# An attention and gated-update kernel: token tiles split in token order and turned by DMA, x added in the last stage, and GpSimd adding both pairs of probability tiles in odd units only

## The reference, cut to what matters

```python
x = x + attention(layernorm(x), ctx, ctx)          # 32 query heads, 8 key heads, softmax over 512 keys
y = layernorm(x)
# ffn(y): gates over 8 experts, the largest one wins; a rank-8 update of y by its matrices
x = x + ((1 - gate) * y + gate * (bias + degen @ (update.T @ (y - debias))))
```

## Time and profile before

| | |
|---|---|
| median of three runs | 1025.13 us (1024.51 to 1025.3) |
| profiled execution: span from the first to the last instruction | 1023.9 us (no time beside the span is given for it) |
| TensorE matmul busy | 949.4 us, 93% |
| VectorE busy | 904.8 us, 88% |
| GpSimd busy | 794.4 us, 78% |
| ScalarE busy | 761.3 us, 74% |
| mean granted TensorE clock | 0.992 |
| DMA | 319876 packets, 164.19 MB, 182216 of them under 512 B |

### The profile page before, as it was taken

How to read it: one execution, slowest core, us unless ns; L and a number is a source line. 1 busy time by engine, 2 the same in 40 slices (tenths; PEclk the granted TensorE clock), 3 DMA queues, 4 the chain that set the end, 5 groups by cost and what they waited for, 6 DMA issues and landing times.

```text
span 1023.9 us, 24706 instructions
## 1 busy us (share of the span) xinstructions
PE 949.4 (93%) x9518; PEld 372.5 (36%) x9518; DVE 904.8 (88%) x1138; ACT 761.3 (74%) x1333; POOL 794.4 (78%) x422
## 2 busy tenths in 40 slices
PE   4789999999999999999999999999999999999996
PEld 3223233333333232333333333332222226777773
DVE  6869999999999999999999999998888876888976
ACT  7468888888888888888888888888777777554440
POOL 7158999999999999999999999998999998222110
PEclk9989999999999999999999999999999999999998
DMA  7675677767677767676767686766555744766423
GB/s 247 184 167 114 161 154 168 156 162 159 155 158 167 168 152 170 145 171 150 180 143 175 138 188 134 182 122 154 119 119 139 165 95 141 247 213 236 148 104 164
DMA packets 319876, 164.19 MB, mean 160 GB/s; under 512 B 182216, under 2 KB 307240, under 8 KB 319760
## 3 DMA queue, kind: packets, MB, share of 16 engines
q1 hardware_dynamic: 319456, 161.76, 64.3%
q0 software_dynamic: 304, 0.85, 0.3%
HBM read 107.58 MB, written 54.53 MB: 158 GB/s over the span
## 4 chain that ended last, share of the span: by engine, by line
PE 36%; DVE 30%; issue 25%; ACT 5%; POOL 2%; DMA 1%; SPq 0%; DVEq 0%; POOLq 0%; ACTq 0%
DVE row_max L949 14%; PE psum L589 8%; PE psum L603 6%; PE psum L616 5%; PE psum L734 5%; DVE den_t L961 4%; PE psum L551 4%; ACT probs L884 3%; PE psum L712 3%; DVE o_t L955 3%; PE psum L577 2%; DVE probs L1161 2%; DVE prod_mem L1008 2%; PE psum L700 1%; ACT prod_mem L824 1%
## 5 line engine op out<-in xcount | busy, mean ns | idle before, releaser
L884 ACT ACTIVATE probs<-psum 128x512 f32<-128x512 f32 x1024 | 554.7, 596 | 106.7 <-PE psum L589 88.7
L949 DVE TENSOR_REDUCE row_max<-psum 128x4 f32<-128x2048 f32 x248 | 566.0, 2282 | 63.5 <-PE psum L551 63.1
L589 PE MATMUL psum<-q_stack,k_stack 97*32 97x512 f16 x4096 | 335.0, 386 | 10.2 <-issue 3.6
L363 POOL TENSOR_TENSOR sums<-probs 128x2048 f32<-128x2048 f32 x63 | 287.8, 4568 | 19.5 <-ACT probs L884 19.5
L351 POOL TENSOR_TENSOR sums<-probs 128x2048 f32<-128x2048 f32 x63 | 287.2, 4558 | 10.2 <-PE psum L626 5.5
L603 PE MATMUL psum<-probs,v_in 128*32 128x512 f32 x2048 | 268.9, 598 | 1.0
L589 PEld LDWEIGHTS psum<-q_stack,k_stack 97*32 97x32 f16 x4096 | 96.8, 95 | 258.7 <-ACT probs L884 148.6
L551 PE MATMUL psum<-high_mem 32*128 32x512 f16 x992 | 98.3, 385 | 23.7 <-DVE row_max L949 20.0
L323 POOL TENSOR_TENSOR o_t<-o_t,inv 128x512 f32<-128x512 f32 x64 | 67.1, 1048 | 44.2 <-DVE inv L967 44.2
L328 POOL TENSOR_TENSOR o_all<-o_all,o_t 128x512 f32<-128x512 f32 x64 | 81.5, 1274 | 9.5 <-POOL o_t L323 0.4
L603 PEld LDWEIGHTS psum<-probs,v_in 128*32 128x32 f32 x2048 | 59.4, 111 | 61.1 <-issue 16.7
(11 more groups left out here) (120 smaller groups left out, 788.9 us busy)
## 6 DMA issues: line engine op xcount, KB each, us to landing
q_stack<-q_split SPq DMA_DIRECT2D x192, 128.0 KB, 3.4
xa<-in_x_dram SPq DMA_DIRECT2D x32, 512.0 KB, 4.7
o_all<-in_x_dram SPq DMA_DIRECT2D x256, 64.0 KB, 2.5
x_attended<-o_all SPq DMA_DIRECT2D x64, 256.0 KB, 4.1
out_dram<-probs SPq DMA_DIRECT2D x32, 512.0 KB, 2.9
q_split<-prod_mem SPq DMA_DIRECT2D x15, 1024.0 KB, 5.4
xa<-x_attended SPq DMA_DIRECT2D x16, 512.0 KB, 4.5
probs<-x_attended SPq DMA_DIRECT2D x16, 512.0 KB, 5.3
```

Source lines behind the costliest of these rows:

```text
L363: pool.tensor_tensor(sums[:, 2 * u % SUMS], probs[:, u % 2, 0], probs[:, u % 2, 1], ALU.add).then_inc(front_done, 1)
L589: last = pe.matmul(st_ps[row:row + D, bank_of["score", u, n], :], k_stack[:, u % SLOTS, t * P + row:t * P + row + D], q_stack[:, u % SLOTS ...
L884: act.activation(probs[:, s, keys, g, :], st_ps[:, bank_of["score", u, n], :], ACT.Exp, scale=EXP_SCALE).then_inc(exped, 1)
L949: dve.reduce_max(row_max[:, u % 2, t:G * ST:ST], s_ps[:], AX.X).then_inc(reduced, 1)
```

## The change

- **Tiles from the sixth on** (n = 5 to 31) no longer go through TensorE and PSUM. ScalarE scales and rounds the context (`split_context`), normalises x in place in one pass (`normalise_tile`) and copies it to f16 (`high_part`), at fixed places among the exponentials: before numbers 4 and 6 of even units and 2 of odd ones. GpSimd subtracts for the low parts (`low_parts`) and also makes the scaled mean. SP turns the f16 tiles with two transposing DMAs, `turn_c` and `turn_x`.
- **x is added in the last stage.** `normalise` only multiplies, into `o_all`. GpSimd's `add_x` adds a tile of x, loaded by `load_addend` with one DMA of 512 KB, before the statistics of that tile. In its loop over the last stage `add_x(n + 2)` stands ahead of `row_root(n)`.
- **Sums.** In odd units GpSimd adds both pairs of probability tiles. In even ones it adds tiles 0 and 1, and TensorE sums three groups of four matmuls: tile 2, the sum, tile 3. There are two buffers of sums for three.
- **Order.** Each quarter has four scores. `turn_max` stands at the head of quarter 2, ahead of `score_rows`; gathers stand in quarters 0, 2 and twice in 3. The denominators of an odd unit are computed in quarters 1 and 2 of the next, those of an even one in quarters 0 and 1; `take_denominators` follows `largest` in the second of these quarters. The planner counts 8 uses for a denominator where it counted 5. Six tiles are loaded ahead, and the buffers are laid out anew.

The diff, cut to the parts that are spoken of; of most functions only the new lines stand, and the old ones are those of the listing above:

```diff
-            BANKS, SUMS = 3, 3
+            BANKS, SUMS = 3, 2
...
+            summed_twice = lambda u: u % 2 == 1 and u < UNITS - 1
+            sums_of = lambda u, half: sums[:, (u + u // 2 + half) % SUMS]
+            den_quarters = lambda u: (1, 2) if summed_twice(u) else (0, 1)
...
+            C_SPLIT_AT, CENTRE_AT, HIGH_AT, SHIFT_AT = 4, 6, 2, 8
...
-                    scores = [("score", u, n) for n in range(BEGIN[u % 2][t], BEGIN[u % 2][t + 1])] if live(u) else []
-                    half = MIDST[u % 2][t] - BEGIN[u % 2][t]
-                    if u % 2 == 1 and t < PIECES and whole(tile_of(u)):
-                        filled.append(("part", tile_of(u), t))
-                    filled += scores[:half]
                     if t == 2 and live(u + 1):
                         filled.append(("max", u + 1, 0))
-                    filled += scores[half:]
-                    if t == (ST - 1 if u % 2 == 1 else 2) and live(u - 1):
+                    if live(u - 1) and t == den_quarters(u - 1)[0]:
                         filled.append(("den", u - 1, 0))
-            KEPT = {"score": 2, "max": 2, "den": (5, 5), "part": 6}
+                    if live(u):
+                        filled += [("score", u, n) for n in range(G * t, G * (t + 1))]
+            KEPT = {"score": 2, "max": 2, "den": 8, "part": 2}
...
-                if use[0] == "part" and use[1] >= FIRST and use[2] > 0:
-                    bank = bank_of["part", use[1], use[2] - 1]
...
+                def low_parts(n):
+
+                    pool.wait_ge(c_high, n - FIRST + 1)
+                    pool.tensor_scalar(c_tile(n), c_tile(n), UP, None, ALU.mult).then_inc(c_scaled, 1)
+                    turned(pool, n - 2, "c")
+                    pool.wait_ge(c_scaled, 2 * (n - FIRST) + 1)
+                    pool.tensor_tensor(c_parts(n)[:, 1], c_tile(n), c_parts(n)[:, 0], ALU.subtract
+                                       ).then_inc(c_scaled, 1)
+                    turned(pool, n - 2, "x")
+                    pool.wait_ge(x_high, n - FIRST + 1)
+                    pool.tensor_tensor(x_parts(n)[:, 1], x_tile(n), x_parts(n)[:, 0], ALU.subtract
+                                       ).then_inc(low_done, 1)
...
+                    pool.tensor_tensor(o_all[:, half, :, h, :], o_t[:, u % 2].rearrange("p (a d) -> p a d", d=D),
                                        inv[:, u % 2].unsqueeze(2).to_broadcast([P, S // D, D]),
+                                       ALU.mult).then_inc(o_made, 1)
+
+                def add_x(n):
+
+                    q, k, t = n // ST, n // ST % GROUPS, n % ST
+                    pool.wait_ge(t_in[ST * k + t], 16 * (q // GROUPS + 1))
+                    if n < EARLY * ST:
+                        pool.wait_ge(add_in[n % 2], 16 * (n // 2 + 1))
+                    else:
+                        pool.wait_ge(add_in[2 + (n - EARLY * ST) % 3], 16 * ((n - EARLY * ST) // 3 + 1))
+                    attended = xa[k][:, t].rearrange("p (g h d) -> p g h d", g=G, h=KV)
+                    pool.tensor_tensor(attended, attended, x_addend(n).rearrange("p (h g d) -> p g h d", h=KV, g=G),
+                                       ALU.add).then_inc(added, 1)
...
+                for u in range(-AHEAD, UNITS + 1):
+                    if u % 2 == 0 and whole(tile_of(u)) and u > -AHEAD:
+                        inverse_root(tile_of(u))
+                    if u % 2 == 1 and whole(tile_of(u)):
+                        low_parts(tile_of(u))
+                    if summed_twice(u - 1) and u > 0:
                         wait(pool, exped, NSC * u)
                         wait(pool, den_done, u - 1)
+                        pool.tensor_tensor(sums_of(u - 1, 1), probs[:, (u - 1) % 2, 2], probs[:, (u - 1) % 2, 3],
+                                           ALU.add).then_inc(back_done, 1)
                     if u == UNITS - 1:
                         for t in range(ST):
                             row_root(0, 0, t)
                     if 0 <= u < UNITS - 1:
                         wait(pool, exped, NSC * u + NSC // 2)
+                        if summed_twice(u - 1) and u > 0:
+                            pool.wait_ge(den_begun, u // 2)
+                        else:
+                            wait(pool, den_done, u - 1)
+                        pool.tensor_tensor(sums_of(u, 0), probs[:, u % 2, 0], probs[:, u % 2, 1],
                                            ALU.add).then_inc(front_done, 1)
+                    if u == UNITS:
+                        add_x(EARLY * ST - 1)
+                        row_root(1, 1, 0)
+                        row_root(1, 1, 1)
+                    if live(u - 1):
+                        normalise(u - 1)
+                    if 0 <= u - 1 - (UNITS - KV) < EARLY * ST - 1:
+                        add_x(u - 1 - (UNITS - KV))
 
                 for n in range(ST + 2, TILES):
+                    if n + 2 < TILES:
+                        add_x(n + 2)
...
+                def turn_x(n):
+
+                    sp.wait_ge(low_done, n - FIRST + 1)
+                    if n % 2 == 0:
+                        sp.wait_ge(split_out, stored(n // 2))
+                    sp.dma_start_transpose(q_parts_of(n)[:, :, :, n % 2 * P:(n % 2 + 1) * P]
+                                           .rearrange("p l h s -> p (l h) s"),
+                                           x_parts(n).rearrange("p l e -> p (l e)")).then_inc(turned_in["x"][n % 2], 16)
...
+                    if u % 2 == 1 and whole(n):
+                        turn_c(n)
+                    if u % 2 == 0 and (n - 1) % 2 == 1 and whole(n - 1):
+                        store_split(n - 1)
+                    if live(u - 2) and (u - 2) % HALF == HALF - 1:
+                        store_half(u - 2)
+                    if u % 2 == 0 and n + UPFRONT - 1 < TILES and u > -AHEAD:
+                        load_x(n + UPFRONT - 1)
+                    if live(u) and live(u + 1):
                         send_shift(u + 1)
+                    if u % 2 == 1 and whole(n):
+                        turn_x(n)
...
+                        if ST * (q + EARLY) + t < TILES:
+                            load_addend(ST * (q + EARLY) + t)
...
+                def denominators(u, i):
+
+                    if i == 0:
+                        bank_free("den", u, 0)
+                    if summed_twice(u):
+                        terms = (sums_of(u, 0), sums_of(u, 1))[i]
+                        if i == 0:
+                            pe.wait_ge(front_done, u + 1)
+                        else:
+                            pe.wait_ge(back_done, (u + 1) // 2)
+                        last_group = 1
                     else:
+                        terms = (probs[:, u % 2, 2], sums_of(u, 0), probs[:, u % 2, 3])[i]
+                        if i == 1:
+                            pe.wait_ge(front_done, u + 1)
+                        else:
+                            pe.wait_ge(exped, NSC * u + (G * 3, 0, NSC)[i])
+                        last_group = 2
                     for g in range(G):
                         last = pe.matmul(st_ps[g * D:(g + 1) * D, bank_of["den", u, 0], :], ones[:, 0:D],
+                                         terms[:, g, :], start=(i == 0), stop=(i == last_group))
+                    if i == last_group:
+                        last.then_inc(den_done, 1)
+                    elif i == 0 and summed_twice(u):
+                        last.then_inc(den_begun, 1)
...
+                        if t == 2 and live(u + 1):
+                            turn_max(u + 1)
                         if 0 <= maxima_at(u, t)[0] < HALVED:
                             first_rows(*maxima_at(u, t))
                         elif live(maxima_at(u, t)[0]):
                             score_rows(*maxima_at(u, t))
                         if (u, t) in DOWN_AT:
                             turn_down(DOWN_AT.index((u, t)))
                         if (u, t) == FOLD_AT:
                             fold_constants()
+                        if live(u - 1) and live(u):
+                            for i in range(2):
+                                if t == den_quarters(u - 1)[i]:
+                                    denominators(u - 1, i)
+                        if t == ST - 1 and live(u):
+                            gather(u, 1)
                         if live(u):
+                            score_keys(u, G * t, G * t + 2)
+                        if t == 0 and live(u - 1):
+                            gather(u - 1, ST - 1)
+                        if t == 1 and live(u - 1) and live(u) and not summed_twice(u - 1):
+                            denominators(u - 1, 2)
+                        if t == 2 and live(u):
+                            gather(u, 0)
+                        if t == ST - 1 and live(u):
+                            gather(u, 2)
+                        if live(u):
+                            score_keys(u, G * t + 2, G * (t + 1))
...
```

(39 more changed lines are left out.)

332 lines of the change are left out of this document (125 added, 207 removed).

## The result

The changed kernel takes 1235.2 us (median of four runs, 1232.0 to 1237.8) against 1024.8 us: ratio 1.205, 95% interval 1.203 to 1.208. The direction was forecast; the 1155 us were 80 too low, and the range ended at 1190. The profiled execution spans 1233.6 us, against 1023.9.

The account below looks back on a forecast made before the run. No engine has room, so the order of the work was taken to bound the kernel. Span 1023.9 + 104 (pairs with tiles) + 20 (without) - 6 (start) + 12 (end) = 1153.9; with 1.2 for the median, 1155 us, range 1080 to 1190.

Parts of the forecast that it names:

- The walk: Attention, two units quarter by quarter: 29.3 us against 25.32, +4.0 a pair, +104 us over 26 pairs.
- Without tiles: Attention pairs with no tiles left: 27.5 us against 24.12, +3.4 a pair, +20 us over six pairs.
- The two waits: Attention: score 9 of even and score 6 of odd units wait for den_t, 2.1 and 0.8 us.
- rival 4: Attention: stalls of 2.1 us lower TensorE's clock a tenth of the time, 64 us more, 1218 us; 5%.
- my 21.9: Attention, inside the clock rival: TensorE's queue in us a pair, which would double at the lower level.
- 2.5 us more a tile fits: Last stage: GpSimd, busy 26.8 of 135 us, has room for each tile's addition; +1 us in all.
- The +11 of the late addend: Start of the last stage: add_x(8), its addend issued behind store_half(63), delays row_root(6); +11 us (0 to +15).
- The start: Before the attention: tile 6's context part leaves TensorE's queue, ending an idle of 3.64 us; -6 us (0 to -9).
- rival 3: Attention: slow DMA transposes make send_shift some 8 us late in one unit of four, +104, 1256 us; 9%.
- the 0 put on the transposes: Attention: the DMA transposes on SP's queue delay no near reader; 0 us, with up to +26.
- 1: Attention: only the two bank waits count, ScalarE's copies stay hidden; 1085 us, 15%.
- 2: Attention: den_t doesn't hold the score back and relief outweighs; 24.3 us a pair, 1004 us, 7%.

Follow-up runs that it names:

- e1: Changed kernel with the planner counting 12 uses instead of 8 for a denominator, so its bank is reused later; 1134.3 us, ratio 1.108.
- b1: Kernel before, planner counting 3 uses instead of 5 for an even unit's denominator, one gather moved behind scores 2 and 3; 1077.6 us, ratio 1.053.
- e17: e14 with x added to o_all in the attention as in the kernel before, but its loads issued one unit earlier; 1092.3 us, ratio 1.068.
- e6: e1 with ScalarE's two passes over a tile cut into halves of 512 columns and spread among the exponentials; 1134.5 us.
- e10: Changed kernel with the edits of e1, e3 and e4, turn_max behind the maximum scores, gather(u, 0) ahead of turn_max, additions in four pieces; 1078.1 us, ratio 1.055.
- e14: e10 with the gather back behind scores 8 and 9, row_root ahead of add_x, and the normalising pass before exponential 8; 1049.3 us, ratio 1.024.
- e4: Changed kernel with the addends of tiles 8 to 10 loaded ahead of store_half(63); 1222.3 us, ratio 1.194.
- e9: e4 with each addition of x cut to 32 of its 1024 columns, loads, waits and order kept; 1199.2 us.
- e15: e4 with each addition replaced by one of 32 columns and two memsets of the addend's slot; 1211.7 us, ratio 1.182.
- e3: Changed kernel with SP sending a unit's shift ahead of store_split, store_half and load_x instead of behind them; 1225.7 us, ratio 1.198.
- e12: e4 with row_root(n) ahead of add_x(n + 2) in GpSimd's loop over the last stage; 1224.3 us.

## Why the prediction was wrong

- **The walk was right, by a little luck.** The quarters were forecast as 2.82, 4.77, 5.03, 2.92, 3.03, 4.9, 2.83, 3.0 and measured, at the higher clock, as 2.84, 4.8, 5.05, 3.05, 3.2, 4.52, 2.92, 2.93: 29.3 us each; the 0.38 by which one is too long and the 0.09 to 0.17 by which three are too short cancel. Without tiles: 27.5 forecast, 28.1 measured. That a bank held too long makes scores wait for den_t is shown by e1. The two waits were put at 2.1 and 0.8 us; removing them shortened their quarters by 1.92 and 0.40.
- **The clock is the first step that failed.** I took it as 1.00 all through the attention and gave rival 4 only 5%. A pair is 1.44 us longer than its walk (24 pairs), one without a tile 0.97 (5 pairs): 39 us, half of the error. Rival 4 itself had the effect, not the place or the size: it looked for the fall behind the stalls for den_t and priced a tenth of the time at 64 us. The clock fell behind turn_max's wait of 1.31 us, was low for 16% of the attention, and cost 39, since a part of it lay in the wait for den_t. What spoke against rival 4, that TensorE is short of work again and again at 1.00 before, was seen in a kernel with 24.35 of 25.3 us busy. I carried it over to one in which it is busy 23.85 of 29.3 us in a pair without a fall (my 21.9 has no working). But b1 and e17 show that neither the busy share nor the longest idle alone decides. The Trainium skill (TensorE: Matmul & The Clock Gate, A second HAM failure mode: psum-queue depth-cycling), named in the prediction, says that frequent idles between groups of matmuls make the clock swing, and by that rival 4 was to come true. The trace agrees for the changed kernel, and b1, e6, e10 and e14, which have such idles and keep the clock in the attention, limit it.
- **The last stage's "2.5 us more a tile fits"** (+1) measured 25 us (e4 against e9), another third, and failed as well. I counted GpSimd's free time alone. A part of what the additions took was VectorE's, whose chain of small operations to the gates TensorE waits for once in four tiles: 10 of the 25 us went when GpSimd no longer read (e15), and how the rest divides is open. The +11 of the late addend was right (e4: 11.0).
- **The start** came out at +10.8 for -6. The late shift that rival 3 looked for in one unit of four came once, at the start, where store_split stands close behind the first transposes. Of the 16.8 us of error, 7.6 are this shift (e3), and the other 9 are not explained. In the attention the late shifts cost 3.6 us at most (e3), and e14's attention with all its transposes is shorter than before, so the 0 put on the transposes there was right.
- **Sum of the errors:** start 16.8, walk -5, clock 39, end 28, together 79, against 1233.6 - 1153.9 = 79.7.

Of the rivals, 1 fell (the copies did cost), 2 too as stated; but e14 shows its idea to be sound once the bank and the pass are both moved: 24.9 us a pair against its 24.3. Three of the prediction's sums are slightly off, and nothing hangs on them: GpSimd's terms add up to 20.2 us, not 20.6, and rival 3's 1153.9 + 104 and + 26 to 1258 and 1180, not 1256 and 1178.

## What to carry to other kernels

Forecasting stalls, forecast what they do to the clock: that a kernel shows idles at the higher level says little about the same idles in another order of work. Look for the fall of the clock ahead of the stall you blame, at the first matmuls that take twice their time. A lower clock costs only where it outlasts the wait that is there anyway. Free time on GpSimd is not free if its instruction reads two tensors from SBUF beside a chain of small VectorE operations; look at who runs beside it, not at its own share. When the largest wait of a stage can be removed at no gain (e12), the next one stood right behind it: test by leaving the work out (e9) before mending its order.

## What was not expected of the hardware

- One wait of 1.59 us on TensorE in each pair leaves the clock at 1.00 (b1), while waits of 0.56 and 0.94 us, after rows as busy, go with the lower level in most pairs (e17).
- The clock is low for 147 us of the attention of the changed kernel and costs 39: where the slow matmuls only fill a wait, they are free.
- A VectorE operation of 128x32 takes 2.22 us instead of 0.19 when it starts just after the start of a GpSimd addition of 2.35 us.
- The transposing DMA of 512 KB held SP's queue for 4.44 us at 57.12 (1.8 at the least, 2.6 in the median of 27), where the plain loads of a tile in the start took up to 1.3. In the attention, where no near reader stands behind it, no loss by it was measured.
